# A graph layer's last phase: VectorE forms two normalisation factors early in a step instead of at its end

## The chip, the cores and the metric

The kernel runs on one core of a Trainium2 chip. The metric is the device time of one execution in microseconds. A core has five engines with queues of their own: TensorE (PE; its weight loads are listed as PEld), VectorE (DVE), ScalarE (ACT), GpSimd (POOL) and SyncE (SP, which here only starts DMAs). Each engine takes its instructions in program order; an instruction that waits for a semaphore holds back everything behind it on its engine.

## The reference

A two-layer graph network with a residual and a layer norm. Nodes: 100,000 rows of 256 numbers; edges: 25,000 (source, destination) pairs, sorted by destination.

```
mean = segment_sum(x[src], dst) / max(degree, 1)
h1   = relu(mean @ W1_l + b1 + x @ W1_r)
mean = segment_sum(h1[src], dst) / max(degree, 1)
h2   = relu(mean @ W2_l + b2 + h1 @ W2_r)
out  = layernorm(x + h2 @ W3 + b3)          # per row, eps 1e-5
```

Only destinations of edges have a mean that is not zero. So the kernel computes all rows once without the mean part, and afterwards computes the destinations' rows anew with it and overwrites them in the output.

## The kernel before, in words

Rows are worked on in groups of 512 (4 tiles of 128 rows): 196 groups of nodes, 49 groups of edge slots. The matmuls are in a high part and a low part of each 32-bit operand: ScalarE rounds a tile to its high part (`..._hi`), VectorE subtracts it from the tile to get the low part (`..._lo`), and TensorE adds up three products (hi·hi, hi·lo, lo·hi).

There are two phases. The first goes over the 196 groups of nodes (function `body`, line 790 on VectorE) and, mixed into it, gathers for the edges. The **last phase** is the one that the change touches: `step(j, b, left)`, run for the 49 groups j of edge slots by `edge_passes` (five steps written out, ten rounds of a loop of four steps, four steps written out). `b` is j modulo 2 and chooses one of two buffers. The work on one group of slots is spread over several steps and engines. In step j, in the order of each engine's program:

- **TensorE**: transposes of the destinations' h1 rows of group j+1 (`turn_hd`, line 901); 24 matmuls of 512 columns for the second layer of group j (`columns`, line 910), which wait for the low part of the mean, `xt_lo` (made by VectorE one step earlier); 24 matmuls of 256 columns for the third layer of group j−1 (`last_layer`, line 921), which wait for `h_lo` of j−1 and for `y` of j−2.
- **VectorE**: `y` of j−2 (third layer plus x and bias, line 625; it waits for the third layer's matmuls and for `o` of j−4); `h_lo` of j−1 (`low_second`, line 837; it waits for `h_hi`); `mean` of j+1 (line 772); `xe_lo` of j+1 (line 778); the sums for mean and variance of `y` of j−2 (`stats`, four instructions, line 631); `xt_lo` of j+1 (line 782; it waits for `xt_hi`); mean and variance of j−2 (`mv`, four instructions, line 638); then the **factors** of j−3: `rs` = 1/sd (RECIPROCAL, line 643, waits for `sd`) and `nb` = −mean·rs (line 645, waits for `rs`).
- **ScalarE**: `xe_hi` of j+1 (line 525), `xt_hi` of j+1 (line 529, waits for `mean`), the normalised output `o` of j−3 (four instructions, line 574, waits for `nb` and for the scatter of j−5, which has used the same buffer), bias and relu of group j in two halves (line 557, each waits for its half of the second layer), `h_hi` of j (line 561), the standard deviation `sd` of j−2 (line 565, waits for `mv`).
- **GpSimd**: four scatters of `o` to the rows of the output (line 467) for each group.
- **SyncE**: the loads for the coming steps (`xn` from `h_tab` and from `run_tab`, `src_h` from `seg_tab`, `xb` from `xdb_tab`); each waits until its buffer has been read (`xb` of j for `y` of j−2).

In steps 0 to 2 the groups of the first phase that are still under way are finished (`residual_rows`, `factors_rows`, and in steps 0 and 1 two scans, line 760, with their transposes). Step 48 (`left` is 0) has no coming group and finishes groups 46 to 48 after its own work. The order on every engine is the one in which the code is written; nothing reorders it.

Of the kernel before, what the change touches and what calls it, by code (L numbers as in the profile page):

```python
# [13 lines left out]
def build(nc, x, src, dst, W1_l, b1, W1_r, W2_l, b2, W2_r, W3, b3, out):  # L14
# [5 lines left out]
    NG = -(-N // G)  # L20
# [15 lines left out]
    with ExitStack() as ctx:  # L36
# [165 lines left out]
        def early(j, n):  # L202
            return isinstance(j, int) and j < n
# [400 lines left out]
        def _(dve):  # L604
# [11 lines left out]
            def low_h(g, n, h, ps):  # L616
                dve.wait_ge(hhi_ok[n], g + 1)
                nc.vector.tensor_tensor(h_lo[:, h], ps[:, :, :], h_hi[:, h].bitcast(f32), ALU.subtract).then_inc(hlo_ok[n], 1)  # L618
# [9 lines left out]
            def sums_of(g, b, y_s, stats_s):  # L628
                dve.wait_ge(y_s, g + 1)
                for s in range(S):  # L630
                    ins = nc.vector.bn_stats(stats[:, s], y[:, b, s])  # L631
                ins.then_inc(stats_s, 1)

            def averages(g, b, stats_s, mv_s):
                dve.wait_ge(w_hi_ok, 1)
                dve.wait_ge(stats_s, g + 1)
                for s in range(S):
                    ins = nc.vector.bn_aggr(mv[:, b, s], stats[:, s])  # L638
                ins.then_inc(mv_s, 1)

            def factors(g, b, sd_s, rs_s, nb_s):
                dve.wait_ge(sd_s, g + 1)
                nc.vector.reciprocal(rs[:, b], sd[:, b]).then_inc(rs_s, 1)
                dve.wait_ge(rs_s, g + 1)
                nc.vector.scalar_tensor_tensor(nb[:, b], mv[:, b, :, 0], -1.0, rs[:, b], ALU.mult, ALU.mult).then_inc(nb_s, 1)  # L645

            def residual_rows(g, b, ps):
                dve.wait_ge(xb_ok, g + 1)
                after(dve, o_ok, g - 1)
                residual(g, b, l3_ps, y_ok, ps)  # L650
# [5 lines left out]
            def factors_rows(g, b):  # L656
                factors(g, b, sd_ok, rs_ok, nb_ok)
# [93 lines left out]
            def sum_up_again(j, b, k, ps):  # L751
                dve.wait_ge(mask_in[b], slot_use(j, b))
                dve.wait_ge(hs_ps, j * K + k + 1)
                if not early(j, 1):
                    dve.wait_ge(hs_ok, j * K + k - 1)
                if early(j, 1):
                    dve.wait_ge(mean_ok, NE)
                elif not early(j, 2):
                    dve.wait_ge(run_out[b], slot_use(j - 2, b))
                nc.vector.tensor_tensor_scan(run[:, b, k], seg[:, b], ps[:, k], run[:, 1 - b, k, G - 1:G], ALU.mult, ALU.add)\  # L760
                    .then_inc(hs_ok, 1)
# [6 lines left out]
            def means(j, b):  # L768
                dve.wait_ge(c_run_in[b], slot_use(j, b))
                dve.wait_ge(c_deg_in[b], slot_use(j, b))  # L770
                after(dve, c_mlo_ok, j)
                nc.vector.tensor_tensor(mean[:, :, :], xn[:, b].rearrange("p s d -> p (s d)").rearrange("p (k g) -> p k g", k=K),  # L772
                                        deg_of[:, b * G:(b + 1) * G].unsqueeze(1).to_broadcast([P, K, G]), ALU.mult)\
                    .then_inc(c_mean_ok, 1)

            def low_hd(j, b):
                dve.wait_ge(c_hdhi_ok, j + 1)
                nc.vector.tensor_tensor(xe_lo[:, b], pair[0][:, :, :], xe_hi[:, b].bitcast(f32), ALU.subtract).then_inc(c_hdlo_ok, 1)  # L778

            def mean_low(j, b):  # L780
                dve.wait_ge(c_mhi_ok, j + 1)
                nc.vector.tensor_tensor(xt_lo[:, b], mean[:, :, :], xt_hi[:, b].bitcast(f32), ALU.subtract).then_inc(c_mlo_ok, 1)
# [52 lines left out]
            def low_second(j, b):  # L835
                dve.wait_ge(c_hhi_ok, j + 1)
                nc.vector.tensor_tensor(h_lo[:, b], pair[1 + b][:, :, :], h_hi[:, b].bitcast(f32), ALU.subtract).then_inc(c_hlo_ok, 1)  # L837

            def residual_edges(j, b):
                dve.wait_ge(c_xb_in[b], slot_use(j, b))  # L840
                if early(j, 2):
                    dve.wait_ge(o_ok, NG - 1 + j)
                after(dve, c_o_ok, j - 1)
                residual(j, b, c_l3_ps, c_y_ok, pair[3])

            def sums_edges(j, b):
                sums_of(j, b, c_y_ok, c_stats_ok)

            def averages_edges(j, b):
                averages(j, b, c_stats_ok, c_mv_ok)  # L850

            def factors_edges(j, b):
                factors(j, b, c_sd_ok, c_rs_ok, c_nb_ok)

            def step(j, b, left):
                g = NG - 2 + j if early(j, 2) else None
                if g is None:
                    residual_edges(j - 2, b)
                else:
                    residual_rows(g, g % 2, pair[1] if j == 0 else pair[3])  # L860
                if early(j, 1):
                    low_h(NG - 1, 1, 2, pair[3])
                else:
                    low_second(j - 1, 1 - b)
                if left:
                    means(j + 1, 1 - b)
                    low_hd(j + 1, 1 - b)
                if g is None:
                    sums_edges(j - 2, b)
                else:  # L870
                    sums_of(g, g % 2, y_ok, stats_ok)
                if left:
                    mean_low(j + 1, 1 - b)
                if g is None:
                    averages_edges(j - 2, b)
                else:
                    averages(g, g % 2, stats_ok, mv_ok)
                if early(j, LEFT):
                    n = NE - LEFT + j
                    for k in range(K):  # L880
                        sum_up_again(n, n % 2, k, pair[0])
                if early(j, 3):
                    if j:
                        factors_rows(NG - 3 + j, (NG - 3 + j) % 2)
                else:
                    factors_edges(j - 3, 1 - b)
                if not left:
                    low_second(j, b)
                    factors_edges(j - 2, b)
                    for n, c in ((j - 1, 1 - b), (j, b)):  # L890
                        residual_edges(n, c)
                        sums_edges(n, c)
                        averages_edges(n, c)
                        factors_edges(n, c)
            edge_passes(dve, step)

        @block.tensor
# [225 lines left out]
```

## Time and profile before

| | us |
|---|---|
| median of three runs | 2983.49 (2982.53 to 2984.09) |
| profiled execution | 2981.34 |
| its span in the trace | 2979.3 |
| TensorE busy over the span | 2867.0 (96%) |
| VectorE busy | 2303.6 (77%) |
| ScalarE busy | 1953.8 (66%) |
| GpSimd busy | 1778.7 (60%) |
| steady part of the last phase (steps 3 to 47) | 2450.2 to 2926.8 in the trace |

All times below are from the span's start. The busy shares are of the whole span; the last phase is about a sixth of it and has shares of its own. A "busy" TensorE counts a matmul until its modelled end, and matmuls overlap, so the distance from one matmul's start to the next says more than the duration. In a row, the bracket [2.20 <-ACT o L574] means that the engine stood idle 2.20 us before the instruction and that ScalarE's write of `o` (line 574) ended this. Buffer numbers are left out of the names.

### The profile page before, as it was taken

The numbers are of one execution on the slowest core, as the hardware profiler recorded it, in microseconds if no ns is written. First come the engines' busy times: TensorE is split into PE (matmuls) and PEld (weight loads), VectorE is DVE, ScalarE is ACT, GpSimd is POOL, SyncE is SP. The second block draws the span as 40 slices with busy tenths as digits, with TensorE's granted clock in tenths as the row PEclk, the third lists the DMA queues.
The fourth block names the chain that finished last, engine by engine and source line by source line (L and its number), as shares of the span: only waits on it lengthen the run. The fifth ranks groups of instructions, "written<-read, shape, count | busy, mean of one in ns | idle before, by whom it ended". The sixth has DMA issues, their size and how long they took to land.

```text
span 2979.3 us, 54466 instructions
## 1 busy us (share of the span) xinstructions
PE 2867.0 (96%) x18457; PEld 2583.0 (87%) x18457; DVE 2303.6 (77%) x4050; ACT 1953.8 (66%) x2994; POOL 1778.7 (60%) x1437
## 2 busy tenths in 40 slices
PE   7999999999999999999999999999999989888895
PEld 6999999999999999999888888888888877777774
DVE  6777877777787777777678888888888867777774
ACT  5666666666666666666677777777777745555554
POOL 5666666766666666666556666666666624444444
PEclk8999999999999999999999999999999999999998
DMA  4555555556555555555445555554555556666652
GB/s 152 170 195 175 187 188 172 185 172 199 173 185 185 169 189 172 195 180 179 145 137 167 180 183 182 169 173 169 178 183 183 178 199 223 215 216 216 212 209 106
DMA packets 274123, 539.63 MB, mean 181 GB/s; under 512 B 39979, under 2 KB 167374, under 8 KB 274074
## 3 DMA queue, kind: packets, MB, share of 16 engines
q1 hardware_dynamic: 223898, 439.17, 44.2%
q0 software_dynamic: 50176, 99.91, 9.6%
q8 instruction: 19, 0.31, 0.0%
q14 instruction: 30, 0.25, 0.0%
HBM read 310.16 MB, written 231.91 MB: 182 GB/s over the span
## 4 chain that ended last, share of the span: by engine, by line
PE 75%; DVE 7%; ACT 6%; issue 6%; POOL 4%; DMA 1%; SPq 0%; DVEq 0%; ACTq 0%; POOLq 0%
PE pair L910 34%; PE pair L921 32%; PE pair L901 10%; ACT o L574 3%; DVE stats L631 2%; DVE mean L772 2%; ACT pair L557 2%; DVE xe_lo L778 2%; ACT h_hi L561 2%; POOL xb L373 1%; POOL xe L414 1%; POOL slots L402 1%; DVE mv L638 1%; DMA xn<-h_tab 0%; DVE nb L645 0%
## 5 line engine op out<-in xcount | busy, mean ns | idle before, releaser
L485 ACT ACTIVATE pair<-pair,bias 128x512 f32<-128x512 f32 x784 | 515.6, 664 | 654.2 <-PE pair L910 654.2
L618 DVE TENSOR_TENSOR h_lo<-pair,h_hi 128x1024 fp32r<-128x1024 f32 x392 | 478.7, 1221 | 323.8 <-ACT h_hi L487 322.9
L373 POOL TENSOR_TENSOR xb<-xn,b_row 128x1024 f32<-128x1024 f32 x196 | 469.5, 2396 | 328.6 <-DVE y L625 312.3
L921 PE MATMUL pair<-w_hi,h_hi 128*128 128x256 f32 x1960 | 562.7, 287 | 25.1 <-DVE h_lo L837 16.7
L921 PE MATMUL pair<-w_lo,h_hi 128*128 128x256 f32 x1960 | 557.6, 285 | 0.0
L921 PE MATMUL pair<-w_hi,h_lo 128*128 128x256 f32 x1960 | 557.4, 284 | 0.0
L497 ACT ACTIVATE o<-y,nb,rs 128x256 f32<-128x256 f32 x784 | 407.5, 593 | 93.3 <-DVE nb L645 89.8
L390 POOL DMA_INDIRECT xe<-in_x_dram,idx x392 | 382.8, 976 | 138.7 <-issue 96.7
L625 DVE TENSOR_TENSOR y<-pair,xb 128x1024 f32<-128x1024 f32 x245 | 298.6, 1219 | 199.1 <-ACT o L574 104.7
L467 POOL DMA_INDIRECT out_dram<-o,idx x196 | 235.7, 1202 | 327.2 <-ACT o L574 278.8
L921 PEld LDWEIGHTS pair<-w_hi,h_hi 128*128 128x128 f32 x1960 | 378.6, 193 | 49.1 <-DVE h_lo L837 36.1
L910 PE MATMUL pair<-xt_hi,w_hi 128*128 128x512 f32 x980 | 403.4, 412 | 4.6 <-DVE y L625 4.6
L487 ACT CAST h_hi<-pair 128x1024 fp32r<-128x1024 f32 x392 | 397.4, 1014 | 12.3
L910 PE MATMUL pair<-xt_lo,w_hi 128*128 128x512 f32 x980 | 385.7, 394 | 0.0
L910 PE MATMUL pair<-xt_hi,w_lo 128*128 128x512 f32 x980 | 383.5, 391 | 0.0
L921 PEld LDWEIGHTS pair<-w_lo,h_hi 128*128 128x128 f32 x1960 | 378.6, 193 | 3.6
L921 PEld LDWEIGHTS pair<-w_hi,h_lo 128*128 128x128 f32 x1960 | 378.6, 193 | 0.0
L402 POOL DMA_INDIRECT slots<-slot_tab,idx x196 | 185.6, 947 | 283.1 <-DVE h_row L766 237.2
L631 DVE BATCH_NORM_STATS2 stats<-y 128x6 f32<-128x256 f32 x980 | 343.8, 413 | 6.7
L910 PE MATMUL pair<-h_hi,w_hi 128*128 128x512 f32 x784 | 308.9, 394 | 5.0 <-DVE xt_lo L614 5.0
L910 PE MATMUL pair<-h_hi,w_lo 128*128 128x512 f32 x784 | 308.5, 394 | 0.0
L910 PE MATMUL pair<-h_lo,w_hi 128*128 128x512 f32 x784 | 307.4, 392 | 0.0
(116 smaller groups left out, 6363.4 us busy)
## 6 DMA issues: line engine op xcount, KB each, us to landing
xn<-in_x_dram SPq DMA_DIRECT2D x196, 512.0 KB, 4.1
out_dram<-o SPq DMA_DIRECT2D x196, 512.0 KB, 4.6
seg<-seg_tab SPq DMA_DIRECT2D x49, 512.0 KB, 6.4
xdb_tab<-xdb SPq DMA_DIRECT2D x49, 512.0 KB
h_tab<-src_h SPq DMA_DIRECT2D x49, 512.0 KB
h_tab<-dst_h SPq DMA_DIRECT2D x49, 512.0 KB, 5.1
run_tab<-run SPq DMA_DIRECT2D x49, 512.0 KB, 5.1
xn<-run_tab SPq DMA_DIRECT2D x49, 512.0 KB, 4.1
```

Source lines behind the costliest of these rows:

```text
L373: nc.gpsimd.tensor_tensor(xb[:, b], xn[:, u], b3_row[:, :].unsqueeze(1).to_broadcast([P, S, D]), ALU.add).then_inc(xb_ok, 1)
L390: nc.gpsimd.indirect_dma_start(out=xe[:, kind, s], out_offset=None, in_=x, in_offset=bass.IndirectOffsetOnAxis(ap=idx[:, kind, c:c + 1], a ...
L467: nc.gpsimd.indirect_dma_start(out=out, out_offset=bass.IndirectOffsetOnAxis(ap=idx[:, 2, c:c + 1], axis=0), in_=o[:, b, s], in_offset=Non ...
L485: nc.scalar.activation(ps[:, k], ps[:, k], ACT.Relu, bias=bias[:, n, k:k + 1]).then_inc(hf_ok[n], 1)
L487: nc.scalar.copy(h_hi[:, h], ps[:, :, :]).then_inc(hhi_ok[n], 1)
L497: ins = nc.scalar.activation(o[:, b, s], y[:, b, s], ACT.Identity, bias=nb[:, b, s:s + 1], scale=rs[:, b, s:s + 1])
L618: nc.vector.tensor_tensor(h_lo[:, h], ps[:, :, :], h_hi[:, h].bitcast(f32), ALU.subtract).then_inc(hlo_ok[n], 1)
L625: nc.vector.tensor_tensor(y[:, b].rearrange(flat), ps[:, :, :].rearrange("p k g -> p (k g)"), xb[:, b].rearrange(flat), ALU.add).then_inc( ...
L631: ins = nc.vector.bn_stats(stats[:, s], y[:, b, s])
L901: ins = nc.tensor.transpose(ps[:, k, s * P:(s + 1) * P], rows_of[:, s, k * P:(k + 1) * P], ident[:, :])
L910: ins = nc.tensor.matmul(ps[:, m], wx[:, w, k, m * P:(m + 1) * P], a[:, k], start=first, stop=end)
L921: ins = nc.tensor.matmul(ps[:, s // 2, s % 2 * D:(s % 2 + 1) * D], a[:, k, s * P:(s + 1) * P], wx[:, w, k], start=first, stop=end)
```

## The change

In `step` of VectorE's program the factors of group j−3 (of the first phase's groups in steps 1 and 2) move from behind the mean and variance of j−2 to directly behind `h_lo` of j−1. Two instructions per step change their place, with their waits; nothing is added or taken away, and the other engines' programs are the same, row for row.

```diff
@@ -862,6 +862,11 @@
                     low_h(NG - 1, 1, 2, pair[3])
                 else:
                     low_second(j - 1, 1 - b)
+                if early(j, 3):
+                    if j:
+                        factors_rows(NG - 3 + j, (NG - 3 + j) % 2)
+                else:
+                    factors_edges(j - 3, 1 - b)
                 if left:
                     means(j + 1, 1 - b)
                     low_hd(j + 1, 1 - b)
@@ -879,11 +884,6 @@
                     n = NE - LEFT + j
                     for k in range(K):
                         sum_up_again(n, n % 2, k, pair[0])
-                if early(j, 3):
-                    if j:
-                        factors_rows(NG - 3 + j, (NG - 3 + j) % 2)
-                else:
-                    factors_edges(j - 3, 1 - b)
                 if not left:
                     low_second(j, b)
                     factors_edges(j - 2, b)
```

VectorE's queue in one steady step before (step 3; every step to 47 has these rows, here from `y` on):

```order
L625 TENSOR_TENSOR y<-pair,xb 128x1024
L837 TENSOR_TENSOR h_lo<-pair,h_hi 128x1024
L772 TENSOR_TENSOR mean<-xn,src_h 128x1024
L778 TENSOR_TENSOR xe_lo<-pair,xe_hi 128x1024
L631 BN_STATS stats<-y 128x6 x4
L782 TENSOR_TENSOR xt_lo<-mean,xt_hi 128x1024
L638 BN_AGGR mv<-stats 128x2 x4
L643 RECIPROCAL rs<-sd 128x4
L645 SCALAR_TENSOR_TENSOR nb<-mv,rs 128x4
```

and now:

```order
L625 TENSOR_TENSOR y<-pair,xb 128x1024
L837 TENSOR_TENSOR h_lo<-pair,h_hi 128x1024
L643 RECIPROCAL rs<-sd 128x4
L645 SCALAR_TENSOR_TENSOR nb<-mv,rs 128x4
L772 TENSOR_TENSOR mean<-xn,src_h 128x1024
L778 TENSOR_TENSOR xe_lo<-pair,xe_hi 128x1024
L631 BN_STATS stats<-y 128x6 x4
L782 TENSOR_TENSOR xt_lo<-mean,xt_hi 128x1024
L638 BN_AGGR mv<-stats 128x2 x4
```

`rs` and `nb` stand in front of five groups of instructions that they stood behind; `mean`, `xe_lo`, `stats`, `xt_lo` and `mv` are each two short instructions later in the queue.

In step 1, where the scans stand, VectorE's queue differs in the same way (the lines with + are now, those with − before):

```order
 L625 TENSOR_TENSOR y<-pair,xb 128x1024
 L837 TENSOR_TENSOR h_lo<-pair,h_hi 128x1024
+L643 RECIPROCAL rs<-sd 128x4
+L645 SCALAR_TENSOR_TENSOR nb<-mv,rs 128x4
 L772 TENSOR_TENSOR mean<-xn,src_h 128x1024
 L778 TENSOR_TENSOR xe_lo<-pair,xe_hi 128x1024
...
 L638 BN_AGGR mv<-stats 128x2 x4
 L760 SCALAR_TENSOR_TENSOR run<-seg,run,pair 128x512 x2
-L643 RECIPROCAL rs<-sd 128x4
-L645 SCALAR_TENSOR_TENSOR nb<-mv,rs 128x4
```

Here the factors also pass the two scans of line 760.

## Rows read from the trace of the kernel before

**Rows 1.** Busy time by stretch; columns in the first line, PEclk is TensorE's granted clock.
```profile
core 0: us, PE busy (x) PEld busy (x) DVE busy (x) ACT busy (x) POOL busy (x), PEclk, DMA share, GB/s
...
1600.00:1900.00 300.00, 300.00 (x1857) 267.45 (x1856) 251.13 (x480) 236.16 (x371) 190.37 (x153) 1.00 0.53 179
...
2430.00:2450.00 20.00, 20.00 (x128) 18.01 (x127) 15.98 (x26) 8.43 (x12) 0.00 (x0) 1.00 0.71 237
2500.00:2600.00 100.00, 89.95 (x521) 75.58 (x520) 71.56 (x138) 58.40 (x92) 45.61 (x38) 1.00 0.61 215
```

**Rows 2.** Waits from 2455 to 2945: total us, times, longest us.
```profile
ACT o L574 <- DVE nb L645: 140.3, 45, 3.1
DVE y L625 <- ACT o L574: 104.7, 45, 2.4
...
PE pair L910 <- DVE xt_lo L782: 32.9, 45, 1.6
PE pair L921 <- DVE h_lo L837: 16.7, 46, 0.4
```

**Rows 3.** Timeline of VectorE, one step: start, duration, instruction, [idle before <-releaser].
```profile
2456.18 1.22 DVE L837 TENSOR_TENSOR h_lo<-pair,h_hi 128x1024 fp32r<-128x1024 f32 x1 [0.88 <-ACT h_hi L561]
2457.33 1.22 DVE L772 TENSOR_TENSOR mean<-xn,src_h 128x1024 f32<-128x1024 f32 x1
...
2460.90 1.21 DVE L782 TENSOR_TENSOR xt_lo<-mean,xt_hi 128x1024 fp32r<-128x1024 f32 x1
2462.03 0.37 DVE L638 BATCH_NORM_AGGREGATE mv<-stats 128x2 f32<-128x6 f32 x4
2462.32 0.14 DVE L643 RECIPROCAL rs<-sd 128x4 f32<-128x4 f32 x1
2462.50 0.16 DVE L645 SCALAR_TENSOR_TENSOR nb<-mv,rs 128x4 f32<-128x4 f32 x1
2464.92 1.23 DVE L625 TENSOR_TENSOR y<-pair,xb 128x1024 f32<-128x1024 f32 x1 [2.26 <-ACT o L574]
2467.03 1.23 DVE L837 TENSOR_TENSOR h_lo<-pair,h_hi 128x1024 fp32r<-128x1024 f32 x1 [0.88 <-ACT h_hi L561]
```

**Rows 4.** Timeline of ScalarE in the same step.
```profile
2456.05 0.30 ACT L565 ACTIVATE sd<-mv,eps 128x4 f32<-128x4 f32 x1
2456.25 1.01 ACT L525 CAST xe_hi<-pair 128x1024 fp32r<-128x1024 f32 x1
2458.57 1.05 ACT L529 CAST xt_hi<-mean 128x1024 fp32r<-128x1024 f32 x1 [1.32 <-DVE mean L772]
2462.76 2.08 ACT L574 ACTIVATE o<-y,nb,rs 128x256 f32<-128x256 f32 x4 [3.13 <-DVE nb L645]
2464.74 1.21 ACT L557 ACTIVATE pair<-pair,bias_c 128x512 f32<-128x512 f32 x2
2465.98 1.02 ACT L561 CAST h_hi<-pair 128x1024 fp32r<-128x1024 f32 x1
```

**Rows 5.** Timeline of TensorE in step 2, which it runs without a wait.
```profile
2440.95 1.03 PE L901 MATMUL pair<-ident,xn 128*128 128x128 f32 x8
...
2447.31 0.28 PE L921 MATMUL pair<-w_hi,h_hi 128*128 128x256 f32 x1
...
2450.19 1.03 PE L901 MATMUL pair<-ident,xn 128*128 128x128 f32 x8
```

**Rows 6.** Line 901 from 2445 to 2945: count, ns min/median/max, first and last start.
```profile
L901 PE MATMUL pair<-ident,xn x360: 271/273/273, 2450.2 to 2926.8; 128*128 128x128 f32 x180
```

**Rows 7.** Timelines of VectorE and GpSimd in the tail.
```profile
2951.06 1.22 DVE L837 TENSOR_TENSOR h_lo<-pair,h_hi 128x1024 fp32r<-128x1024 f32 x1 [4.36 <-ACT h_hi L561]
...
2955.59 0.98 POOL L467 DMA_INDIRECT out_dram<-o,idx  x1 [1.01 <-ACT o L574]
...
2969.76 0.98 POOL L467 DMA_INDIRECT out_dram<-o,idx  x1 [0.30 <-issue]
```

**Rows 8.** Line 467 (scatters), last phase: from issue to landing.
```profile
DMA to landing us min/median/max: 2.4/4.2/5.8
```

## The prediction

> **What bounds the kernel now.** I read the busy time by stretch first. The share of 96% that TensorE has over the whole span is not that of the last phase: between 2500 and 2600 us it is busy 89.95 of 100 us, while between 2430 and 2450, in the phase's first steps, it is busy all of the time, at the same granted clock of 1.00, its higher level [rows 1]. So in the steady steps something makes TensorE wait. The waits say what: it waits for `xt_lo` and for `h_lo` of VectorE, 0.73 and 0.36 us per step by modelled ends; ScalarE's `o` waits 3.1 us per step for `nb`, and VectorE's `y` waits 2.3 us for `o` [rows 2]. These form one loop, which the two timelines let one follow round. VectorE runs from `h_lo` at 2456.18 to `nb` at 2462.50 without a gap, with `nb` last [rows 3]. ScalarE's `o` starts 0.26 later, at 2462.76; behind it in ScalarE's queue stand relu (2464.74) and `h_hi` (2465.98), neither of which shows an idle time before it [rows 4]; then `h_lo` of the next step starts at 2467.03 [rows 3]. Sum: 6.32 + 0.26 + 1.98 + 1.24 + 1.05 = 10.85 us. The steady step from the transposes is (2926.8 − 2450.2) / 44 = 10.83 us (360 transposes, 8 in each of 45 steps) [rows 6]. So the loop is the step: no engine is full, and `nb` is the link through which VectorE's whole step and ScalarE's `o`, relu and `h_hi` stand one behind the other.
>
> **What the change does to this loop.** Two instructions per step move; none is added or removed. `rs` and `nb` take 2462.32 to 2462.66, 0.34 us with the wait between them [rows 3].
>
> At the new place RECIPROCAL waits for `sd` of j−3, and `mean`, `xe_lo`, `stats`, `xt_lo` and `mv` are queued behind it. In this row's step `sd` runs from 2456.05 to 2456.35 [rows 4], and `h_lo`, which now stands in front of the factors, from 2456.18 to 2457.40 [rows 3]: `sd` is 1.05 us early, since ScalarE issues it right behind the `h_hi` for which `h_lo` waits anyway. I cost this wait at nothing; `h_lo` is the cover. Without that cover, the bound is `sd`'s own 0.30.
>
> Behind the factors everything on VectorE comes 0.34 later, up to `mv`, and `y` does not, as the factors are gone from the step's end. `xt_lo` is waited for by TensorE, so if nothing else changed the 0.34 would cost a step that much; the lower bound is zero, if TensorE comes to `xt_lo` later than it is ready.
>
> `o` no longer waits for the step's end. The loop now runs `h_lo` to the next item 1.15, factors 0.34, `mean` to `xt_hi` 1.24 [rows 3, 4], `xt_hi` 1.05 (it stands in front of `o` in ScalarE's queue and waits for `mean`), `o` to relu 1.98, relu to `h_hi` 1.24, `h_hi` to `h_lo` 1.05 [rows 4 and 3]: 8.05 us. VectorE's own work, `h_lo` to the end of `nb` 6.48 plus `y` 1.23, is 7.71 [rows 3]; ScalarE's is about 6.5 (`xe_hi` 1.01, `xt_hi` 1.05, `o` 1.98, relu 1.24, `h_hi` with `sd` about 1.2) [rows 4].
>
> **What is late next: TensorE.** Its step without a wait is shown once: from the transposes at 2440.95 to those at 2450.19 in step 2, 9.24 us, columns up to 6.36 and third layer from there [rows 5]. That is above 8.05, 7.71 and 6.5. I go through its waits at that pace, with 0 at the transposes of step j. The third layer of j−2 has just ended, so `y` starts at about 0.3 and ends at 1.5; `h_lo` of j−1 ends at 2.7, long before the third layer wants it at 6.4. Factors to 3.0, `mean` to 4.1, then `xe_lo`, `stats` and `xt_lo` of j+1 follow at VectorE's distances (2457.33 to 2462.03 is 4.70 from `mean`'s start to the end of `xt_lo` [rows 3]), and `xt_lo` is ready at 7.7; the columns of j+1 want it at 9.24 + 0.8 = 10.0. So the 0.34 falls into a slack of 2.3 us and costs nothing. `o` runs from 5.2 to 7.2, relu of j (second half of the columns done at 6.4) to 8.4, `h_hi` to 9.4; `h_lo` of j starts behind `y` at 9.24 + 1.5 = 10.7. The smallest slack is this last one, 1.3 us. So the step is TensorE's.
>
> The Trainium skill bears on how much TensorE has to give ("Perfetto Trace Analysis", section "Identifying the Most-Contended Engine"): matmul busy time is a poor measure, as matmuls are pipelined; the share of weight loads is the better one. By the busy share the steady step could fall only to 10.83 × 0.8995 = 9.74; by weight loads, 75.58 per 100 us here against 18.01 per 20 us where TensorE never waits [rows 1], to 10.83 × 75.58 / 90.05 = 9.09. The row of start-to-start times, 9.24, lies close to the second, so the trace agrees with the page.
>
> I take 9.24, a measured step with the same instructions; bounds are 9.09 by the weight loads and 9.74 by the waits with modelled ends (10.83 − 1.09 [rows 2]).
>
> **The sum.** Steady part: 44 × (10.83 − 9.24) = 70.0 us. Steps 0 to 2: TensorE is already busy 20.00 of 20 us [rows 1], so the factors' move past the two scans is worth nothing there: 0. The tail: in the old trace 2926.8 is the start of the last destinations' transposes, `h_lo` of group 48 starts 24.3 us later, and from 4.5 us behind that, at 2955.59, twelve scatters are issued back to back, 1.29 apart, to 2969.76 [rows 6, 7]; the time after that is landing and end. The order behind `h_lo` of 48 is not changed, so the tail moves with it. New: `h_lo` of 48 waits for its columns, which end at 9.24 + about 5.6 (6.36 less the transposes) = 14.8, plus a half relu, `h_hi` and latencies, about 1.9: 16.8. Gain 24.3 − 16.8 = 7.5. Together 77.5. The profiled execution took 2981.34 us (its span of 2979.3 and 2.0 around it): 2981.3 − 77.5 = 2903.8. The median shown is 2.15 above the profiled execution, so the forecast is 2906 us.
>
> Other queues: SyncE's `xb` load waits for `y`, which comes earlier, and the loads of `xn` stand behind it; all have a step or more before they are read. GpSimd needs 4 × 1.29 = 5.2 [rows 7] of 9.24.
>
> **Rivals.**
>
> *TensorE's step is longer than the one shown* (forecast's mechanism, other size). The step of 9.24 had no scatter beside it: POOL has 0.00 between 2430 and 2450 [rows 1]. With scatters, and transfers of 10.83 × 215 GB/s = 2.33 MB per step, a pace of 9.24 needs 252 GB/s; the fully busy stretch shows 237. At 237 a step is 9.82. Either way some 9.75 to 9.8: 44 × 1.05 + 6.5 = 53, so about 2931. Against it: in the phase before, TensorE is busy 300.00 of 300 us with GpSimd busy 190 beside it [rows 1], and loads are issued a step or more ahead.
>
> *Transfers don't go faster at all* than 215 GB/s: the step stays at 10.83, and only part of the tail is gained: 2976 to 2983. For it: the stretches differ little from 215. Against: 237 at a DMA share of 0.71 [rows 1].
>
> *The removed wait is replaced by another on `o`*: `o` of j−3 also waits for the scatter of j−5, in the same buffer. At 9.24 per step `o` of j−5 ends 11.3 before the transposes; GpSimd's four issues take 5.2 and its start up to 1.5 more (my allowance), 6.7, landing 4.2 (at most 5.8) [rows 7, 8]: it is there at +1.2 at the latest, and `o` starts at 5.2. **This is the rival on the slower side**: this ring of two steps is 2.1 (`o`) + 6.7 + landing, and it sets the step from a landing of 9.7 us on; above 12.9 it makes the step longer than 10.83. If the denser transfers brought landings of 14, the step would be 11.4, 44 × 0.57 = 25 us more: about 3008. For it, only that scatters now start in another place relative to the loads; against it, no landing above 5.8.
>
> *The change is hidden*: `o` is earlier but relu still waits, as for the columns. That would be the forecast again, for it is TensorE that relu then waits for.
>
> **Chances and range.** Forecast 0.74 (its own range 2898 to 2915: steps of 9.09 to 9.4); longer TensorE step 0.17 (2915 to 2932); transfers at the old rate 0.05 (half of it within the bound); slower ring 0.02; the remaining 0.02 for something slower unseen. Range: 2897 (all steps at 9.09: 44 × 1.74 + 7.5 = 84.1, 2899, less 2 for the spread of runs) to 2932. I count as no change what lies within 0.2%, 6 us, which is about what a measurement of this kernel can tell. Faster 0.93, same 0.03, slower 0.04.
>
> **What would show it.** Right: ScalarE's wait for `nb` and VectorE's for `o` vanish from the waits of the last phase; VectorE waits instead for the third layer's matmuls before `y`; distances of the transposes near 9.24; TensorE without idle from step 3 to 47; weight loads near 0.89 of the stretch. Wrong: TensorE still waiting for `xt_lo` (the 0.34 counts), RECIPROCAL idle for `sd` with `mean` late (the cover is gone), `o` idle for a scatter, or transposes waiting for the loads of `xn`. If the transposes stand at 9.7 or more with TensorE never idle, the step that I took is the term that was wrong.

## The result and the profile after

The changed kernel takes 2901.00 us (median of four runs, 2900.21 to 2902.52) against 2983.01 (2981.65 to 2984.09) for the kernel before, run with it: a ratio of 0.9726, 95% interval 0.9709 to 0.9743. That is 82 us less; 2906 was forecast.

The page of the changed kernel gives the span and the busy time of each engine:

```profile
span 2898.9 us, 54466 instructions
...
PE 2838.0 (98%) x18457; PEld 2580.3 (89%) x18457; DVE 2307.1 (80%) x4050; ACT 1955.5 (67%) x2994; POOL 1738.3 (60%) x1437
```

The work of VectorE and ScalarE is what it was (2303.6 and 1953.8 before); only the span is shorter. Busy time by stretch in the last phase (columns as in [rows 1]):

```profile
2500.00:2600.00 100.00, 100.00 (x612) 89.67 (x611) 83.55 (x165) 69.16 (x110) 43.73 (x44) 1.00 0.69 248
```

TensorE is busy throughout, where it was busy 89.95 [rows 1]: 612 matmuls in 100 us instead of 521 recorded, weight loads 89.67 instead of 75.58, and the transfers have risen from 215 to 248 GB/s. The waits from 2500 to 2800 (total us, times, longest us) show what the change was to remove:

```profile
POOL out_dram L467 <- ACT o L574: 139.9, 33, 4.6
ACT xt_hi L529 <- DVE mean L772: 67.8, 33, 2.3
DVE y L625 <- PE pair L921: 47.5, 33, 1.5
POOL out_dram L467 <- issue: 32.5, 97, 2.3
ACT xe_hi L525 <- PE pair L901: 25.0, 33, 0.9
```

All four rows of [rows 2] are gone: `o` no longer waits for `nb`, `y` no longer for `o`, and TensorE waits for nothing. In their place VectorE waits for TensorE's third layer before `y`, and ScalarE for its transposes before `xe_hi`. One steady step on VectorE (start, duration, instruction, idle time before it), to be held against [rows 3]:

```profile
2605.48 1.23 DVE L625 TENSOR_TENSOR y<-pair,xb 128x1024 f32<-128x1024 f32 x1 [1.45 <-PE pair L921]
2606.62 1.21 DVE L837 TENSOR_TENSOR h_lo<-pair,h_hi 128x1024 fp32r<-128x1024 f32 x1
2607.75 0.17 DVE L643 RECIPROCAL rs<-sd 128x4 f32<-128x4 f32 x1
2607.95 0.20 DVE L645 SCALAR_TENSOR_TENSOR nb<-mv,rs 128x4 f32<-128x4 f32 x1
2608.18 1.23 DVE L772 TENSOR_TENSOR mean<-xn,src_h 128x1024 f32<-128x1024 f32 x1
2609.32 1.22 DVE L778 TENSOR_TENSOR xe_lo<-pair,xe_hi 128x1024 fp32r<-128x1024 f32 x1
2610.45 1.40 DVE L631 BATCH_NORM_STATS2 stats<-y 128x6 f32<-128x256 f32 x4
2611.76 1.21 DVE L782 TENSOR_TENSOR xt_lo<-mean,xt_hi 128x1024 fp32r<-128x1024 f32 x1
```

and the same step on ScalarE, against [rows 4]:

```profile
2604.38 1.01 ACT L561 CAST h_hi<-pair 128x1024 fp32r<-128x1024 f32 x1
2605.29 0.30 ACT L565 ACTIVATE sd<-mv,eps 128x4 f32<-128x4 f32 x1
2606.35 1.02 ACT L525 CAST xe_hi<-pair 128x1024 fp32r<-128x1024 f32 x1 [0.76 <-PE pair L901]
2609.43 1.06 ACT L529 CAST xt_hi<-mean 128x1024 fp32r<-128x1024 f32 x1 [2.07 <-DVE mean L772]
2610.40 2.07 ACT L574 ACTIVATE o<-y,nb,rs 128x256 f32<-128x256 f32 x4
```

`nb` is ready at 2608.15, and `o` starts at 2610.40, straight behind `xt_hi`: it now waits for its turn on ScalarE and not for `nb`. `sd` (ready at 2605.59) is there long before RECIPROCAL (2607.75). `h_hi` is ready at 2605.39, over a microsecond before `h_lo` starts: `h_lo` follows `y`, which follows TensorE.

Where the 80.4 us between the two spans (2979.3 and 2898.9) lie can be read from the starts of the first transposes of groups 4 and 48, which are 44 steps apart. For group 4 before, the row is in [rows 5]; for group 48 before it is

```profile
2926.01 1.04 PE L901 MATMUL pair<-ident,xn 128*128 128x128 f32 x8
```

and for groups 4 and 48 after

```profile
2448.63 1.03 PE L901 MATMUL pair<-ident,xn 128*128 128x128 f32 x8
...
2854.03 1.04 PE L901 MATMUL pair<-ident,xn 128*128 128x128 f32 x8
```

| stretch | before | after | less |
|---|---|---|---|
| up to the transposes of group 4 | 2450.19 | 2448.63 | 1.6 |
| 44 steady steps | 475.82 (10.81 each) | 405.40 (9.21 each) | 70.4 |
| from the transposes of group 48 to the end | 53.3 | 44.9 | 8.4 |

The 1.6 us are not the change's: the last phase's first transposes, which nothing of the change precedes, start at 2407.67 in the trace of before and at 2405.70 in that of after, and in the seven kernels below, whose first phase is the same code, between 2405.9 and 2409.6.

### The profile page after: what moved, and what is told of

Its sections match the earlier page's. It is cut to its first block, busy times and chain, and to the rows that moved or that the text cites. A ratio compares the mean times of both kernels' runs of the same rounds, so it can differ in the third digit from the quotient of the medians.

```text
span 2898.9 us, 54466 instructions
## 1 busy us (share of the span) xinstructions
PE 2838.0 (98%) x18457; PEld 2580.3 (89%) x18457; DVE 2307.1 (80%) x4050; ACT 1955.5 (67%) x2994; POOL 1738.3 (60%) x1437
## 4 chain that ended last, share of the span: by engine, by line
PE 91%; POOL 4%; issue 3%; DVE 1%; DMA 1%; ACT 0%; SPq 0%; POOLq 0%; DVEq 0%; ACTq 0%
PE pair L910 43%; PE pair L921 37%; PE pair L901 11%; POOL xb L373 1%; POOL xe L414 1%; POOL slots L402 1%; DMA xn<-h_tab 0%; POOL out_dram L467 0%; ACT o L574 0%; DVE y L625 0%; DMA xn<-in_x_dram 0%; DVE w_lo L621 0%; DMA xe<-h_tab,h_row 0%; PE pair L987 0%; DMA out_dram<-o,idx 0%
## 5 line engine op out<-in xcount | busy, mean ns | idle before, releaser
L921 PE MATMUL pair<-w_hi,h_hi 128*128 128x256 f32 x1960 | 556.1, 284 | 4.8 <-issue 3.0
L467 POOL DMA_INDIRECT out_dram<-o,idx x196 | 194.1, 990 | 289.9 <-ACT o L574 241.6
```

Source lines behind the costliest of these rows:

```text
L921: ins = nc.tensor.matmul(ps[:, s // 2, s % 2 * D:(s % 2 + 1) * D], a[:, k, s * P:(s + 1) * P], wx[:, w, k], start=first, stop=end)
```

## The experiments

The theory: the old step was the loop `h_lo` – … – `nb` – `o` – relu – `h_hi` – `h_lo`; the change takes `xe_lo`, `stats`, `xt_lo` and `mv` out of it, and TensorE's own 9.21 us became the step. Rivals were that being anywhere but last is enough, that the gain grows evenly with the time by which `nb` is earlier, that the loop of `y` waiting for `o` was the one that counted, that the transfers set the new step, and that what stands ahead of `xt_lo` does. A step's pace below is from starts of transposes, as above: the mean of all 44 steps, and of some 25 to 29 late ones where the first ones differ.

**Factors behind `stats`.** Edit, against the changed kernel:

```diff
                     low_second(j - 1, 1 - b)
-                if early(j, 3):
-                    if j:
-                        factors_rows(NG - 3 + j, (NG - 3 + j) % 2)
-                else:
-                    factors_edges(j - 3, 1 - b)
                 if left:
                     means(j + 1, 1 - b)
...
                     sums_of(g, g % 2, y_ok, stats_ok)
+                if early(j, 3):
+                    if j:
+                        factors_rows(NG - 3 + j, (NG - 3 + j) % 2)
+                else:
+                    factors_edges(j - 3, 1 - b)
                 if left:
                     mean_low(j + 1, 1 - b)
```

> The factors of j-3 stand behind the four stats instructions (ahead of xt_lo), not directly behind h_lo. Theory (loop, then TensorE): the loop from h_lo over nb, o, relu and h_hi back to h_lo is the old 10.85 less xt_lo (1.13) and mv (0.29): 9.43 us, just above TensorE's own 9.21. So steps of about 9.4 to 9.45, 44 x 0.22 = 10 us more than the changed kernel plus about 1 in the tail: about 2912. Rival 1 (it is enough that the factors are not last): 2901. Rival 2 (the gain grows evenly with the time by which nb comes earlier, 4.97 us for 82 us): nb comes 1.4 us earlier, gain 23, about 2959.

Measured: 2915.36 us (2914.53 to 2916.08), ratio to before 0.9775 (0.9758 to 0.9791). From 2600.51 to 2864.53 a step takes 9.43 us, the sum of the loop (that the second digit agrees is partly chance: the sum started from one step of 10.85, and from the old loop's mean of 10.83 over its late steps it would be 9.41). The first steps run at TensorE's 9.21; in each of them `xt_lo` comes 0.2 us later against the transposes, from 7.6 us behind them to 10.4 after 13 steps, and from there on the pace is the loop's. The mean of all is 9.37. The spans differ from the changed kernel's by 14.7: 44 × 0.154 = 6.8 in the steps; 3.7 before step 3, which are there already at the last phase's first transposes (2409.58 against 2405.70) and so aren't the edit's; 4.2 in the tail, where 1 was expected. Of these, 2.7 are the lag that the first steps built up (`h_lo` of group 47 comes 4.17 us behind the transposes of group 48, and 1.44 in the changed kernel); the rest was not followed up. The loop is in the timeline of VectorE and ScalarE, with its two waits back:

```profile
2604.63 1.22 DVE L837 TENSOR_TENSOR h_lo<-pair,h_hi 128x1024 fp32r<-128x1024 f32 x1 [0.77 <-ACT h_hi L561]
...
2609.54 0.16 DVE L645 SCALAR_TENSOR_TENSOR nb<-mv,rs 128x4 f32<-128x4 f32 x1
```
```profile
2609.80 2.08 ACT L574 ACTIVATE o<-y,nb,rs 128x256 f32<-128x256 f32 x4 [1.73 <-DVE nb L645]
```

`h_lo` at 2604.63 to `nb` at 2609.54 is 4.91, `nb` to `o` 0.26: as the sum had it. The busy row of this kernel, from a stretch in which every step is at the loop's pace, is a warning; the row of the changed kernel for the same stretch stands below it:

```profile
2600.00:2700.00 100.00, 99.88 (x592) 87.57 (x591) 80.86 (x159) 68.84 (x109) 51.19 (x42) 1.00 0.68 240
```
```profile
2600.00:2700.00 100.00, 100.00 (x612) 89.67 (x611) 83.50 (x164) 70.06 (x110) 42.35 (x43) 1.00 0.70 251
```

TensorE reads as busy 99.88 of 100 us and yet it isn't the bound; the modelled ends of matmuls cover nearly all of the 0.2 us per step by which its step is longer. The number of matmuls (592 against 612) and the weight loads (87.57 against 89.67, 2.3% less, as 9.21 is 2.3% less than 9.43) show it. The Trainium skill ("Perfetto Trace Analysis", section "Identifying the Most-Contended Engine") calls matmul busy time a poor measure, as matmuls are pipelined, and the share of weight loads the better one; these two rows agree.

**Factors behind `xt_lo`, ahead of `mv`.** The same five lines, put ahead of `averages`:

```diff
                 if left:
                     mean_low(j + 1, 1 - b)
+                if early(j, 3):
+                    if j:
+                        factors_rows(NG - 3 + j, (NG - 3 + j) % 2)
+                else:
+                    factors_edges(j - 3, 1 - b)
                 if g is None:
                     averages_edges(j - 2, b)
```

> The factors of j-3 stand behind xt_lo, ahead of mv, so only mv (0.29 us) is taken out from in front of nb. Theory: loop 10.85 - 0.29 = 10.56, steps of 10.55, 44 x 1.35 = 59 us more than the changed kernel: about 2962, some 20 faster than the kernel before (with steps 0 to 2 and the tail). Rival 1 (not last is enough): 2901. Rival 2 (even growth): gain 5, about 2978.

Measured: 2964.91 us (2962.99 to 2967.27), ratio 0.9943 (0.9926 to 0.996). Late steps 10.56 us (2603.62 to 2909.94, 29 steps), mean 10.48. Taking 0.29 us out from in front of `nb` gives 0.27 us per step (late steps take 10.83 in the kernel before). With the run above this settles the form of the dependence: neither a switch nor even growth, but the length of the loop until it falls to TensorE's step.

**Factors ahead of `h_lo`.**

```diff
                     residual_rows(g, g % 2, pair[1] if j == 0 else pair[3])
+                if early(j, 3):
+                    if j:
+                        factors_rows(NG - 3 + j, (NG - 3 + j) % 2)
+                else:
+                    factors_edges(j - 3, 1 - b)
                 if early(j, 1):
                     low_h(NG - 1, 1, 2, pair[3])
                 else:
                     low_second(j - 1, 1 - b)
```

> The factors of j-3 stand one place earlier than in the changed kernel, between y and h_lo, so that h_lo no longer covers RECIPROCAL's wait for sd. Theory: TensorE sets the step, y waits for it, and sd is ready before y ends (2605.59 against 2606.71 in the changed kernel's trace), so nothing waits: 2901 within 4. Rival (the cover by h_lo is needed): RECIPROCAL waits up to 0.3 us per step with h_lo behind it and TensorE's third layer behind that: up to 44 x 0.3 = 13 more, 2914.

Measured: 2902.17 us (2900.91 to 2903.67), ratio 0.9733 (0.9717 to 0.9749); 9.214 us per step, as in the changed kernel. VectorE's rows show RECIPROCAL behind `y` without a wait, and `h_lo` later:

```profile
2605.69 1.23 DVE L625 TENSOR_TENSOR y<-pair,xb 128x1024 f32<-128x1024 f32 x1 [1.58 <-PE pair L921]
2606.83 0.17 DVE L643 RECIPROCAL rs<-sd 128x4 f32<-128x4 f32 x1
2607.04 0.16 DVE L645 SCALAR_TENSOR_TENSOR nb<-mv,rs 128x4 f32<-128x4 f32 x1
2607.12 1.22 DVE L837 TENSOR_TENSOR h_lo<-pair,h_hi 128x1024 fp32r<-128x1024 f32 x1
```

So the cover by `h_lo`, which the prediction named for the wait on `sd`, isn't needed: once TensorE sets the step, `y` comes late enough.

**ScalarE's order changed instead.** VectorE as before the change; in ScalarE's `step`:

```diff
-                if early(j, 3):
-                    if j:
-                        normalise(NG - 3 + j, (NG - 3 + j) % 2)
-                else:
-                    finish_edges(j - 3, 1 - b)
                 second(j, b, 0)
                 second(j, b, 1)
                 second_high(j, b)
...
                     deviation_edges(j - 2, b)
+                if early(j, 3):
+                    if j:
+                        normalise(NG - 3 + j, (NG - 3 + j) % 2)
+                else:
+                    finish_edges(j - 3, 1 - b)
```

> VectorE's program is that of the kernel before (factors at the step's end). In ScalarE's program o of j-3 moves behind h_hi and ahead of sd of j-2, so relu and h_hi no longer stand behind o; y of j-1 still waits for o of j-3. Theory: the old loop is cut, the next is y, h_lo to nb, o, and back to y: 1.14 + 6.48 + 0.1 + 2.08 + 0.08 = 9.88 us, above TensorE's 9.21. Steps of 9.9, about 2901 + 44 x 0.67 = 2931 to 2940. Rival (the loop that bounded was that of y waiting for o, relu and h_hi behind o were only along): no gain, 2983. Rival (only the early nb helps): 2983.

(In the kernel that ran `o` stands behind `sd` of j−2, not ahead of it as this says.) Measured: 2939.08 us (2938.13 to 2940.28), ratio 0.9856 (0.9839 to 0.9872); late steps 9.94 us, mean 9.91. The second loop is there as summed, but for the link from `o` to `y`: the sum had 2.16 us for it, from one step of the kernel before, and it takes 2.25 on average, in both kernels. With the means of the links the sum is 1.14 + 6.47 + 0.08 + 2.25 = 9.94 us, as measured. `sd` in front of `o` adds nothing: `o` starts 0.1 us behind the end of `nb`. In the step shown, on VectorE and then on ScalarE, `o` to `y` takes 2.27:

```profile
2602.18 1.23 DVE L625 TENSOR_TENSOR y<-pair,xb 128x1024 f32<-128x1024 f32 x1 [2.30 <-ACT o L574]
...
2609.62 0.16 DVE L645 SCALAR_TENSOR_TENSOR nb<-mv,rs 128x4 f32<-128x4 f32 x1
2612.15 1.23 DVE L625 TENSOR_TENSOR y<-pair,xb 128x1024 f32<-128x1024 f32 x1 [2.36 <-ACT o L574]
```
```profile
2609.88 2.08 ACT L574 ACTIVATE o<-y,nb,rs 128x256 f32<-128x256 f32 x4
```

Half of the gain comes with `nb` exactly where it was, from taking relu and `h_hi` out from behind `o`. So it is not the early `nb` as such that pays. Nor was the wait of `y` for `o`, the largest one on VectorE in [rows 2], what bounded the kernel before: there `h_lo` stood idle another 0.88 us behind `y` for `h_hi` [rows 3], and here, where the loop through that wait is the bound, the wait is still 2.3 us and a step is 0.9 us shorter.

**Eight matmuls less, in both kernels.** In the last phase's second layer the product with the low part of the weights is left out (`short` is set only there):

```diff
                         for wx, a in ((w_hi, hi), (w_lo, hi), (w_hi, lo)):
+                            if short and wx is w_lo:
+                                continue
```

On the changed kernel:

> The changed kernel without the low-part-of-the-weights product in the last phase's second layer: 16 matmuls of 512 columns per step instead of 24 (that part of the result is left out). Theory: TensorE sets the step at 9.21; without 8 x 0.2275 = 1.8 us it would be 7.4, so the next bound shows: the loop h_lo, factors, mean, xt_hi, o, relu, h_hi of 8.05 us (VectorE's own work is 7.7). Steps of 8.05 to 8.3, 2901 - 44 x 1.1 = about 2852. Rival (the transfers, at 252 GB/s now, set the step): steps stay at 9.2, 2895 to 2901.

Measured: 2845.9 us (2842.64 to 2846.0), ratio to before 0.9541 (0.9525 to 0.9557); 7.99 us per step over all 44, 8.01 over the late ones. TensorE was the bound, and what is next is the loop of 8.05 us that the prediction had summed; in this step `h_lo` comes back after 7.93 and waits for `h_hi` again:

```profile
2601.84 1.23 DVE L837 TENSOR_TENSOR h_lo<-pair,h_hi 128x1024 fp32r<-128x1024 f32 x1 [0.28 <-ACT h_hi L561]
...
2609.77 1.23 DVE L837 TENSOR_TENSOR h_lo<-pair,h_hi 128x1024 fp32r<-128x1024 f32 x1 [0.28 <-ACT h_hi L561]
```

and its row by stretch shows transfers at 291 GB/s, so that 248 was no limit:

```profile
2500.00:2600.00 100.00, 95.70 (x607) 84.70 (x605) 95.57 (x187) 78.43 (x126) 50.06 (x49) 1.00 0.83 291
```

On the kernel before:

> The kernel before, with the same 8 matmuls per step left out. Theory: its steady step is the loop over nb, o, relu and h_hi, on which no matmul lies: steps stay at 10.83, and only steps 0 to 2, where TensorE is full, give some 2 us each: about 2976. Rival (TensorE's work counts in the kernel before too, its waits being a consequence of when it starts): 44 x 1.8 = 80 us less, about 2900.

Measured: 2979.98 us (2977.57 to 2981.47), ratio 0.9993 (0.9984 to 1.0003): no difference that can be told; 10.82 us per step. The 6 us that were expected of steps 0 to 2 are 2.1 in the traces. The same 8 matmuls are worth 55 us in one kernel and nothing that can be told in the other. Its waits from 2500 to 2780 show where the time went:

```profile
ACT o L574 <- DVE nb L645: 81.1, 26, 3.1
...
PE pair L923 <- DVE h_lo L837: 51.9, 26, 2.2
```

`o` waits for `nb` as long as ever, 3.1 us per step, and TensorE (the line is 923 here) waits 2.0 us for `h_lo` instead of 0.36.

**`stats` issued twice.** On the changed kernel:

```diff
             def sums_edges(j, b):
+                dve.wait_ge(c_y_ok, j + 1)
+                for s in range(S):
+                    nc.vector.bn_stats(stats_x[:, s], y[:, b, s])
                 sums_of(j, b, c_y_ok, c_stats_ok)
```

> The changed kernel with the four stats instructions of each edge group issued twice, the first time into a spare tile: 1.31 us more on VectorE per step, ahead of xt_lo, mv and the next y. Theory: VectorE idles 1.45 us per step before y, and xt_lo has over 2 us in hand, so TensorE's 9.21 still holds: 2901 to 2906. Rival (what stands ahead of xt_lo on VectorE sets when TensorE starts its columns): 44 x 1.31 = 58 more, 2959.

Measured: 2903.53 us (2898.82 to 2905.37), ratio 0.974 (0.9724 to 0.9756); 9.21 us per step, with VectorE at 97.22 of 100 us:

```profile
2500.00:2600.00 100.00, 100.00 (x609) 89.55 (x608) 97.22 (x206) 69.52 (x108) 57.64 (x44) 1.00 0.71 251
```

So 1.31 us more in front of `xt_lo` cost a step nothing, and the 0.34 of the change, in the same place, can't either. VectorE has hardly anything left, though.

## Why the prediction was right

- *The loop bounds the step.* Shown: its length, summed from distances between starts, gives the pace of two other positions of the factors (9.43 and 10.56), and a cut at another link gives the next loop (9.94). Without the eight matmuls the kernel before keeps its step.
- *The wait for `sd` costs nothing.* Right, and by more than was said: even without `h_lo` in front of it.
- *The 0.34 ahead of `xt_lo` falls into slack.* Right: 1.31 more there does too. `xt_lo` is ready 7.7 us behind the transposes, as was worked out (in the step shown 2612.97 against 2605.28); the slack of 2.3 us is 2.7 by the experiment behind `stats`, in which it runs out.
- *TensorE is next, at 9.24.* Right in kind, 9.214 in size: the one step that TensorE ran through without a wait in the old trace was a good measure; with scatters beside it, which that step lacked, TensorE's step is not longer. Of the two bounds, 9.09 by the weight loads came within 0.12; 9.74 by the modelled ends was off by half a microsecond per step, for the reason that the experiment behind `stats` shows.
- *The transfers.* 248 to 252 GB/s come without loads arriving late, and 291 can be had.
- *The sum.* 70.0 was said for the steady part and 70.4 measured, 7.5 for the tail and 8.4 measured. One number was misread: 2926.8 is the start of the last transpose of group 48, while 2450.2 is the first of group 4. The first of group 48 starts at 2926.01, so the old step was 10.81 and not 10.83, and 0.8 us that was counted in the steady part belongs to the tail, which with it comes to 8.3. That the steady part is so close all the same is partly luck: the new step was put too long as well (9.24 for 9.21, 1.1 us over 44 steps), and the two errors nearly cancel. `h_lo` of group 48 was put at 16.8 us behind the transposes and starts 16.6 behind (2870.66 against 2854.03).
- *The remaining 5 us of 2906 to 2901.* The spans differ by 80.4 where 77.5 was forecast, and 1.6 of these 2.9 us lie in the first phase, which the change doesn't touch. The other 2 come from the median: it was put 2.15 us above the profiled execution, and in the new runs it is 0.3 above it (2901.00 and 2900.68).

The rival on the slower side, `o` waiting for the scatter of two groups earlier, is real at one place: the very last `o`. In the tail of the changed kernel, on ScalarE and then on GpSimd:

```profile
2881.47 2.07 ACT L574 ACTIVATE o<-y,nb,rs 128x256 f32<-128x256 f32 x4 [1.28 <-DMA out_dram<-o,idx]
```
```profile
2875.18 0.98 POOL L467 DMA_INDIRECT out_dram<-o,idx  x1 [1.12 <-ACT o L574]
...
2889.37 0.98 POOL L467 DMA_INDIRECT out_dram<-o,idx  x1 [0.30 <-issue]
```

It costs nothing there, for GpSimd issues twelve scatters back to back from 2875.18 and comes to this `o` only after it.

## What to carry to other kernels

When no engine is full, look for a loop through several queues and add up distances from start to start round it; an edit pays by what it takes out of that loop, and only down to the next bound, which should be summed beforehand. A short instruction whose result starts another engine's long chain belongs where its inputs are ready, not at the end of the step in which it was written. A stretch in which the next engine already runs without a wait measured its pace better here, with one step (9.24 for 9.214), than busy time less idle time did (9.74).

## What the runs showed of the hardware that was not expected

- In the kernel before with eight matmuls less, TensorE waits some 2.0 us before the third layer in each step, and its granted clock was 0.93 over 2500 to 2600: after waits of 0.69 and 2.21 us in one step the lower level (1.2 GHz) came in within the third layer, and from 2510.37 us on its matmuls of 256 columns were 0.21 us apart instead of 0.12. In the kernel before, with waits of 0.7 and 0.4 us per step, the clock was 1.00 in all steady steps. The fall cost nothing (10.82 us per step against 10.81), as TensorE wasn't the bound.
- In the kernel before, 9 of the 38 scatter issues from 2500 to 2600 us took 1.97 or 1.98 us instead of 0.98, each the third of a group's four (as at 2500.73 us); in the changed kernel all but one (1.38) of those in the same stretch take 0.98 or 0.99, and GpSimd is busy less (43.73 for 44 issues against 45.61 for 38 [rows 1]) although it does more. With the factors behind `stats` GpSimd is busy 52.80 us for 44 issues in that stretch. What the long ones coincide with was not tried.
